# Moving the far-edge branch of a GNN and attention kernel to behind its eighth chunk

## What is computed

```python
def _L0_gnn_ref(vertex_features, edge_features, edge_index, W1, b1, W2, b2, W3, b3):
    aggr = jax.ops.segment_sum(edge_features, receivers_idx, num_segments=num_vertex)
    collected = jnp.concatenate([vertex_features, aggr], axis=-1)
    h = jax.nn.relu(collected @ W1 + b1)
    h = jax.nn.relu(h @ W2 + b2)
    return h @ W3 + b3
...
x = x + _L0_gnn_ref(_layernorm(x, axis=-1), edge_attr_256, edge_index, ...)
x = x + _L0_ffn_ref(_layernorm(x, axis=-1)[None], ...)[0]
```

## Time and profile before

| | |
|---|---|
| median of 3 runs | 724.66 us (722.9 to 725.93) |
| the profiled execution | 722.99 us, its span 719.9 us |
| TensorE, VectorE, ScalarE, GpSimd busy | 97%, 57%, 42%, 33% of the span |
| HBM read, written | 112.35 MB, 6.40 MB |
| edge stage | 0 to about 287 us |
| handover to the MLP | about 283 to 301 us |

### The profile page before, as it was taken

How to read it: one execution, slowest core, us unless ns; L and a number is a source line. 1 busy time by engine, 2 the same in 40 slices (tenths; PEclk the granted TensorE clock), 3 DMA queues, 4 the chain that set the end, 5 groups by cost and what they waited for, 6 DMA issues and landing times.

```text
span 719.9 us, 12362 instructions
## 1 busy us (share of the span) xinstructions
PE 695.0 (97%) x3520; PEld 433.4 (60%) x3520; DVE 408.1 (57%) x989; ACT 304.2 (42%) x466; POOL 237.7 (33%) x306
## 2 busy tenths in 40 slices
PE   7999999999999999899999989999999999999997
PEld 3666666666666666466556654444444443588886
DVE  6554554555545466153444378888888888522221
ACT  4233333333333334212121225554554454567773
POOL 3101101101101013013332336666666666154442
PEclk9999999999999999999999999999999999999999
DMA  8999999999999996200000003333333333112221
GB/s 313 398 385 416 413 413 410 404 406 405 406 406 404 388 384 222 79 1 0 0 0 0 0 2 59 72 73 71 60 73 73 68 63 73 30 58 73 75 85 64
DMA packets 94976, 131.83 MB, mean 183 GB/s; under 512 B 56681, under 2 KB 70973, under 8 KB 89839
## 3 DMA queue, kind: packets, MB, share of 16 engines
q1 hardware_dynamic: 94143, 131.35, 52.3%
q10 hardware_dynamic: 816, 0.26, 0.2%
HBM read 112.35 MB, written 6.40 MB: 165 GB/s over the span
## 4 chain that ended last, share of the span: by engine, by line
PE 54%; DMA 16%; POOL 13%; issue 12%; DVE 2%; SPq 1%; POOLq 0%; ACT 0%; DVEq 0%; ACTq 0%
DMA ring_mem<-edge_attr_in 16%; PE ps L1116 15%; PE ps L1357 12%; POOL ring_mem L572 7%; POOL ring_mem L580 7%; PE ps L1214 6%; PE ps L1232 6%; PE ps L1222 6%; PE ps L1169 3%; PE ps L1129 2%; PE ps L1161 1%; PE ps L1287 1%; DVE big L824 0%; PE ps L1071 0%; DVE ring_mem L977 0%
## 5 line engine op out<-in xcount | busy, mean ns | idle before, releaser
L1116 PE MATMUL ps<-ring_mem,side 128*64 128x256 f32 x1564 | 186.9, 386 | 7.0 <-DMA ring_mem<-edge_attr_in 4.6
L1116 PEld LDWEIGHTS ps<-ring_mem,side 128*64 128x64 f32 x1564 | 112.4, 137 | 67.3 <-issue 25.5
L741 DVE TENSOR_TENSOR side<-iota_w,rel 128x512 f32<-128x512 f32 x98 | 67.0, 686 | 91.9 <-PE ps L1129 91.7
L634 ACT ACTIVATE side<-ps 128x256 f32<-128x256 f32 (+1 forms) x98 | 40.7, 415 | 143.2 <-PE ps L1116 141.5
L1279 PE MATMUL ps<-ring_mem,xn 128*128 128x512 f32 x196 | 93.4, 599 | 1.8 <-DVE ring_mem L977 1.5
L1287 PE MATMUL ps<-side,ring_mem 128*128 128x512 f32 x196 | 92.3, 593 | 1.0 <-ACT ring_mem L670 1.0
L526 POOL TENSOR_TENSOR var_e<-mv,eps 128x2 f32<-128x2 f32 (+1 forms) x25 | 4.9, 196 | 235.6 <-DVE mv L807 235.6
L824 DVE TENSOR_TENSOR big<-big,ps 128x128 f32 x223 | 63.9, 286 | 30.8 <-issue 12.3
L1357 PE MATMUL ps<-side,ring_mem 128*128 128x256 f32 x360 | 77.9, 379 | 0.0
L580 POOL TENSOR_TENSOR ring_mem<-ring_mem 128x512 f32<-128x512 f32 x49 | 67.3, 1373 | 30.9 <-DVE ring_mem L977 30.9
L1357 PEld LDWEIGHTS ps<-side,ring_mem 128*128 128x128 f32 x360 | 68.4, 190 | 9.3
(11 more groups left out here) (138 smaller groups left out, 824.3 us busy)
## 6 DMA issues: line engine op xcount, KB each, us to landing
ring_mem<-edge_attr_in SPq DMA_DIRECT2D x97, 1024.0 KB, 8.4
x_sb<-x_in SPq DMA_DIRECT2D x24, 256.0 KB, 7.0
result<-ring_mem SPq DMA_DIRECT2D x24, 256.0 KB, 2.1
big<-side SPq DMA_TRANSPOSE x49, 3.1
ring_mem<-edge_attr_in SPq DMA_DIRECT2D x1, 512.0 KB, 5.9
ring_mem<-L_gnn_W_in SPq DMA_DIRECT2D x2, 256.0 KB, 3.5
ring_mem<-L_ffn_W_x_in SPq DMA_DIRECT2D x2, 256.0 KB, 4.5
ring_mem<-L_ffn_W_fx_in SPq DMA_DIRECT2D x1, 512.0 KB, 4.2
```

The lines of the kernel that those rows point to most:

```text
L741: dve.tensor_tensor(hot[:, b], iota_w[:, :].unsqueeze(1).broadcast_to(shape), where.unsqueeze(2).broadcast_to(shape), ALU.is_equal).then_i ...
L1116: last = mm(ps[side_of * WINDOW:(side_of + 1) * WINDOW, SUM_BANKS[s % 2], pair * F:(pair + 1) * F], lhsT=hot[0:parts, s, t, :], rhs=ring8[ ...
```

## The change

1. The far branch moves. `run_chunks` gets a hook `at_far`, called when the peeled front is through. All three engines with a branch call it behind chunk 7 (`FAR_AT = 8`). At the end of the edge stage no engine has a branch any more.
2. The reloading moves from SyncE's program and queue to ScalarE's, which now reads the flag itself; ScalarE's peeled front grows from four chunks to eight.
3. The far edges have buffers of their own in `tmp` (the memory that `h1x` fills later) instead of the ring's slot 0 and `side`, and a semaphore `gen_added` of their own.
4. In TensorE's last chunk the turns of the sums stand before the row transposes.
5. The two W_x blocks are counted on `wx_in`, for which `fold_transposes` waits. The other five stay on `fold_in`, for which TensorE waits before L1249 and VectorE where it did.

```diff
+FAR_AT = 8
-def run_chunks(eng, step, peel_front, last_trip, total, apart=False):
+def run_chunks(eng, step, peel_front, last_trip, total, apart=False, at_far=None):
     for t in range(peel_front * UNROLL):
         step(t, t % UNROLL, t // UNROLL, 1 if apart else 2)
+    if at_far:
+        at_far()
...
-        g_iota = side[:, 0:512]
-        g_hot = part(2048, 2048).rearrange("p (k n) -> p k n", k=UNROLL)
+        far_mem = tmp[:, 7424:12064]
+        far8 = far_mem[:, 0:2048].rearrange("p (t f) -> p t f", t=SUBTILES)
+        g_hot = far_mem[:, 2048:4096].rearrange("p (k n) -> p k n", k=UNROLL)
+        g_iota = far_mem[:, 4096:4608]
...
-                sp.dma_start(wx[k], w_x[k * P:(k + 1) * P, :]).then_inc(fold_in, 16)
+                sp.dma_start(wx[k], w_x[k * P:(k + 1) * P, :]).then_inc(wx_in, 16)
...
-            sp.wait_ge(prep_v, 22)
-            far = sp.value_load(far_i[0:1, 0:1], min_val=0, max_val=1)
...
-            with sp.If(far > 0):
...
-            run_chunks(act, evacuate, 1, EDGE_TRIPS, CHUNKS)
...
+            def far_chunks():
+                act.wait_ge(prep_v, 22)
+                far = act.value_load(far_i[0:1, 0:1], min_val=0, max_val=1)
+                with act.If(far > 0):
+                    with act.Fori(0, WHOLE) as c:
+                        reload(c, 1)
...
+                    reload_last()
+                    act.wait_ge(gen_group, CHUNKS + 1)
+            run_chunks(act, evacuate, FAR_AT // UNROLL, EDGE_TRIPS, CHUNKS, at_far=far_chunks)
...
-            run_chunks(dve, chunk, 2, EDGE_TRIPS - 1, CHUNKS)
-            with dve.If(far_reg[0] > 0):
-                dve.wait_ge(groups_added, CREDIT + ALL_SUMS)
-                dve.wait_ge(fold_t, 1)
+            def far_chunks():
+                with dve.If(far_reg[0] > 0):
+                    dve.wait_ge(groups_added, CREDIT + 2 * FAR_AT)
...
+            run_chunks(dve, chunk, FAR_AT // UNROLL, EDGE_TRIPS - 1, CHUNKS, at_far=far_chunks)
...
-            dve.wait_ge(fold_in, 16 * 7)
+            dve.wait_ge(fold_in, 16 * 5)
...
                 if s % 2 == 0:
                     return
+                if isinstance(c, int) and c == CHUNKS - 1:
+                    turn(c - 1, s - 1, groups)
+                    turn(c, s, groups)
+                    ln_transposes(i - 1, 2)
+                    return
...
-            run_chunks(pe, chunk, 2, EDGE_TRIPS, CHUNKS)
...
+            def far_chunks():
+                with pe.If(far_reg[0] > 0):
+                    pe.wait_ge(win_ready, FAR_AT)
...
+            run_chunks(pe, chunk, FAR_AT // UNROLL, EDGE_TRIPS, CHUNKS, at_far=far_chunks)
             first_layer_x(EDGE_TRIPS - 1, 2, 0)
             first_layer_x(EDGE_TRIPS - 1, 2, 1, bank=4)
             def fold_transposes():
-                pe.wait_ge(fold_in, 16 * 7)
+                pe.wait_ge(wx_in, 16 * KF)
...
             pe.wait_ge(h1x_ready, 2 * (EDGE_TRIPS + 1))
+            pe.wait_ge(fold_in, 16 * 5)
```

More of the change, by code:

```diff
@@ L340, in words, with chunk_rows @@
             return v.bitcast(U16).rearrange("p (n h) -> p h n", h=2)
+        def chunk_rows(c, groups):
+            rows = edges[bass.ds(c * CHUNK_EDGES, CHUNK_EDGES), :]
+            return rows.rearrange("(g p k) f -> p g (k f)", g=groups, p=P) if groups > 1 else rows.rearrange(
+                "(p k) f -> p (k f)", p=P)
         def tiles_of(t0, n):
@@ L347, in _ @@
         def _(sp):
[L350 to L353, removed]
             def slot(s, groups):
@@ new lines, in far_chunks @@
+            def far_chunks():
[4 more added lines that the diff above has]
+                        reload(c, 1)
+                    with act.Fori(WHOLE, PAIRED) as c:
+                        reload(c, 2)
+                    with act.Fori(PAIRED, FULL_CHUNKS) as c:
+                        reload(c, CHUNK_GROUPS)
+                    reload_last()
+                    act.wait_ge(gen_group, CHUNKS + 1)
@@ new lines, in far_chunks, with far_chunk @@
+            def far_chunks():
+                with dve.If(far_reg[0] > 0):
+                    dve.wait_ge(groups_added, CREDIT + 2 * FAR_AT)
+                    for n in range(512 // WINDOW):
+                        dve.tensor_scalar(g_iota[:, n * WINDOW:(n + 1) * WINDOW], iota_w[:, :], float(n * WINDOW), None,
+                                          ALU.add).then_inc(gen_v, 1)
+                    dve.wait_ge(gen_v, 8)
+                    dve.drain().then_inc(gen_group, 1)
+                    PER_CHUNK = 3 + 2 * WIDES
+                    def far_chunk(c, steps):
+                        ahead = c * PER_CHUNK + 8
+                        dve.wait_ge(gen_d_in, c * 16 + (16 if len(steps[1]) == UNROLL else 32))
+                        dve.tensor_copy(g_abs, g_dst).then_inc(gen_v, 1)
+                        dve.tensor_scalar(g_cov, rel[:, bass.ds(c, 1), :].rearrange("p c t -> p (c t)"),
+                                          float(WINDOW), float(4 * AGG), ALU.is_lt, ALU.mult).then_inc(gen_v, 1)
+                        dve.wait_ge(gen_v, ahead + 2)
+                        dve.tensor_tensor(g_abs, g_abs, g_cov, ALU.add).then_inc(gen_v, 1)
+                        for half_of, tiles in enumerate(steps):
+                            for w in range(WIDES):
+                                turn = half_of * WIDES + w
+                                dve.wait_ge(gen_v, ahead + (3 + turn))
+                                dve.tensor_scalar(g_win, g_abs, float(w * WIDE), None, ALU.subtract).then_inc(gen_v, 1)
+                                dve.wait_ge(gen_v, ahead + (4 + turn))
+                                for t in tiles:
+                                    dve.tensor_scalar(g_hot[:, t % UNROLL, :], g_iota, g_win[:, t:t + 1], None,
+                                                      ALU.is_equal).then_inc(gen_hot, 1)
+                                dve.wait_ge(gen_sums, c * (2 * WIDES) + (turn + 1))
+                                view = agg[:, :, w * WIDE:(w + 1) * WIDE]
+                                last = dve.tensor_tensor(view, view, ps[:, 0:2, 0:WIDE], ALU.add)
+                                last.then_inc(gen_added, 1)
+                                dve.wait_ge(gen_added, c * (2 * WIDES) + (turn + 1))
+                        dve.memset(g_cov, 0.0).then_inc(gen_group, 1)
+                    with dve.Fori(0, FULL_CHUNKS) as c:
+                        far_chunk(c, [range(0, UNROLL), range(UNROLL, SUBTILES)])
+                    far_chunk(FULL_CHUNKS, [range(0, UNROLL), range(UNROLL, UNROLL + ROWS_PER_PART)])
```

99 lines of the change are left out of this document (47 added, 52 removed).

## The result

The changed kernel takes 725.68 us (median of 20 runs, 723.43 to 728.19), the kernel before 723.86 us beside it (20 runs, 721.79 to 727.06). The ratio is 1.0024, 95% interval 1.0013 to 1.0035: **slower by 1.8 us**, within the 0.5% that one measurement tells apart, and against the forecast, which was 2.3 us faster. The range given ended at 724.8. The profiled execution of the changed kernel took 726.10 us, 3.1 more than that of the kernel before, and its span, 724.3 us, is 4.4 longer: the pair of profiles overstates the difference by 1.3 to 2.6 us.

What follows compares the result with a forecast made beforehand. The edge stage was taken as DMA-bound, TensorE just behind, with TensorE's waits and slow clock at the handover after it. Handover -4.7, branch +1.0 and clock +1.4 made -2.3 us: 722.4 us on the 724.66 median, range 719.0 to 724.8.

Steps and rivals of the forecast that it cites:

- The handover: Behind the edge stage: first MLP product starts 2.9 us earlier and full clock saves 1.8 us, together -4.7 us.
- The price of the branch amid traffic: At chunk 8: compare holds 3.69 us, TensorE stalls 2.9 us, DMA idles 0.8 us; with 0.2 for traffic, +1.0 us.
- rival (d): At chunk 8: edge transfers starve the fetch, branch holds TensorE 10.6 us, DMA idles 7.6; +4.6 us, 729.3 us; chance 0.07.
- The clock: Around chunk 8: the stall probably lowers TensorE's granted clock, +1.4 us, bounds 0 and 1.7 us.
- What the queue absorbs: At chunk 8: queued transfers let TensorE free a slot up to 2.1 us late before the DMA runs dry.
- the DMA runs dry, once, near 42 us: Sign in the changed kernel's profile: the share of the DMA engines dips once near 42 us; idle time forecast 0.8 us.
- ScalarE and VectorE: At chunk 8: VectorE's 2.7 us jump runs beside TensorE's, ScalarE's flag load takes under 1 us; both cost 0.
- (a): At chunk 8: the stall comes but the clock stays up; -3.7 us, 721.0 us; chance 0.32.
- (b): At chunk 8: nothing is paid, target already held or queue deeper than 2.1 us; -4.7 us, 720.0 us; chance 0.13.
- (c): At the handover: the clock falls all the same, 1.8 us of gain missing; -0.5 us, 724.2 us; chance 0.06.

Runs made afterwards that it cites:

- f4: The kernel before with wx_in alone, so the W_x transposes no longer wait for W_slice; branch and turns stay in place: 720.01 us, ratio 0.9949.
- e2: The changed kernel without wx_in and without the turns before the row transposes, leaving the moved branch: 726.30 us, ratio 1.0034.
- g2: The changed kernel with the far block looped and short on TensorE alone, VectorE keeping its long block and jump: 720.17 us, ratio 0.9941.
- the short block: The changed kernel with the far block's 13 windows in a loop on TensorE and VectorE: 718.88 us, ratio 0.9937.

## Why the prediction was wrong

**The handover** was right: -4.7 us forecast, -5.1 measured, through the same steps. L1232 starts 9.1 us behind the sums of chunk 96, and the forecast had 288.2 - 278.8 = 9.4. The clock stayed up. What the forecast didn't ask is which part of the change earns it: 3.7 us come with the weights' semaphore alone (f4), since the clock then holds even with the long branch in place, and 4.4 with the branch alone (e2). On top of the semaphore the move adds 1.2 us (16.8 for 18.0), and it is the move that costs in the edge stage.

**The price of the branch amid traffic** is the step that failed. The forecast carried the 3690 ns of the earlier trace rows from a stretch where the DMA engines were nearly idle to one where all sixteen were busy, and added 0.2 us. Measured: 6386, 5916 and 6492 ns with edge transfers running, 3442 without them at the same place, 3480 to 3992 at the old place. So the stall was 5.75 us and not 2.9, and the DMA ran dry for 6.3 us and not for 0.8. The mechanism was rival (d), at less than half of its size; the point from which it decides, given as 5.9 us, was passed. It had a chance of 0.07. The row that pointed to it, 8.9 us for 1 KB on another queue, was argued away by its small pieces. The arbitration packet by packet, cited there from the Trainium skill ("DMA: Bandwidth & Descriptors", Queues, rings and completion order), can't alone explain it: the fetch showed no packet at all for 4 us, 1 of which it takes in a quiet stretch too. What it does in those 4 us no trace here shows.

**The clock** fell, as the forecast had it, but for twice the time: 6.8 us at 1.2 GHz in the changed kernel, 3.4 in the one with the branch alone. The forecast's upper bound, one stretch like that at 291 us, was none. As 1.3 of the 6.8 us lie inside the stall, 6.29 - 3.61 = 2.7 us were lost at half speed, against the 1.4 put down. These two terms together are 5.75 + 2.7 = 8.4 us of TensorE's time, and that is what is missing: from chunk 7 to chunk 12 it took 23.3 us (32.58 to 55.89) against 14.8 with the short block.

**What the queue absorbs**, 2.1 us in the forecast, comes out as 8.5 - 6.3 = 2.2 us by the DMA window and as 8.5 - 6.9 = 1.6 by the medians. With the branch alone (e2) the same sums give only 0.8 and 0.2 (7.2 us lost on TensorE, 6.4 by the DMA, 7.0 by the medians), so the size is about right in the changed kernel and isn't shown as a constant. The pair of profiles can't decide it: chunk 96 is 9.4 us later in that of the changed kernel, but in the seven kernels with the branch at its old place the start of chunk 96 varies from 278.8 to 281.5 us, and in the kernel before it is among the earliest. That the DMA runs dry, once, near 42 us was right; the time for which it does was not.

**ScalarE and VectorE** were put at nothing. ScalarE: yes, its compare held 50 ns. VectorE: hidden behind TensorE's stall here, but its 4.5 us (2.7 at the old place) show up as a 1.1 us wait of TensorE once TensorE's own stall is gone (g2).

**Rivals.** (a) and (b) are out, since the compare held and the clock fell. (c) is out: full clock at the handover. On the branch, "Runtime: NRT & Kernel Launch", Instruction fetch mechanics, of the Trainium skill was the rule to go by. The short block agrees with its condition, a target inside what is held: 336 to 368 ns, and no instruction packet. The 108 ns of "Advanced Engine Details and Errata", Control Flow Timing, hold for neither jump on TensorE.

## What to carry to other kernels

A block that is skipped still costs a jump, and in these runs its price lay in its length (two were tried) and in the traffic at that moment: look at the duration of the compare on the engine's sequencer, and loop the block's body so that the skip stays short, before asking where to put it. A stall measured where the DMA engines are idle is not the stall in a stretch that they bound. Don't wait for a transfer on a shared count that the next step doesn't need: that one line was worth 3.7 us, nearly half of it because the engine's clock then stayed up. And if two parts of a change take away neighbouring idle times, measure each alone: their gains need not add.

## What the runs showed of the hardware

- A forward jump over some 400 rows of matmuls and waits held TensorE's sequencer for 3.4 to 4.0 us where the DMA engines' share over the compare was 0.03 to 0.37 (five kernels) and for 5.9 to 6.5 us where it was 0.78 to 1.01 (three kernels); a jump over some 50 rows for 0.34 to 0.37 us, with edge transfers running or not (five kernels).
- Under load, the last instruction packet before the compare let go appeared 3.6 to 4.0 us after the compare's start (three kernels; with the branch behind chunk 15 there was another at 1.7 us), without load 1.0 to 1.2 us after it (five kernels). The packet itself took 0.9 to 1.4 us, and the compare let go 1.4 to 1.5 us after its end in all eight.
- A 5.75 us stall of TensorE in otherwise dense work brought 6.8 us at 1.2 GHz, beginning inside the stall, as did one of 4.97 us; one of 5.3 us brought 3.4 us. At the handover 1.39 and 2.70 us of idleness with 1.3 us of work between them brought a fall, and so did 0.69, 0.41 and 2.48 (the turns alone); 2.08 us alone, 1.59 alone, or 0.69 and 1.67 with 3.1 us of work between them did not.
